# Retention, experts, recurrence, experts on one core: the recurrence's first chunk of returned rows is fetched in the experts' block and taken by halves

## What is computed

```
x = x + attn_a(layernorm(x))          # retention, 16 heads
x = x + ffn(layernorm(x))             # experts, top 2 of 8
x = x + attn_b(layernorm(x))          # recurrence
x = x + ffn(layernorm(x))

# ffn:    acc = sum over the two chosen experts of  weight * (silu(gate) * up) @ w2.T
# attn_b: sx  = shift(x) - x                       # x is the normed input here
#         xxx = x + sx * time_maa_x
#         m   = tanh(xxx @ tm_w1); delta = m @ tm_w2     (five maps)
#         xw, xk, xv, xr, xg = x + sx * (time_maa_wkvrg + delta)
#         r, k, v, g, w from these; scan over tokens; norm by head; * g @ Wo
```

## Time and profile before

| | us |
|---|---|
| median of 3 runs | 1408.81 |
| lowest and highest of them | 1406.04, 1409.01 |
| the profiled execution, its own time | 1404.32 |
| its span in the trace | 1402.5 |
| PE busy | 1148.3 (82%) |
| DVE busy | 907.4 (65%) |
| ACT busy | 617.2 (44%) |
| POOL busy | 547.9 (39%) |

### The profile page before, as it was taken

The page is one execution under the profiler, slowest core; times in us unless marked ns, Lnnn a source line. Parts: engine busy times, 40 slices in busy tenths (PEclk is TensorE's granted clock), DMA queues, the critical chain, the costliest instruction groups (busy, mean ns, idle before and its releaser), DMA issues. The chain is left out here.

```text
span 1402.5 us, 34498 instructions
## 1 busy us (share of the span) xinstructions
PE 1148.3 (82%) x13832; PEld 792.6 (57%) x13832; DVE 907.4 (65%) x1881; ACT 617.2 (44%) x1311; POOL 547.9 (39%) x532
## 2 busy tenths in 40 slices
PE   5999999966399999178989999998987547999960
PEld 3666666644288888124555555555555326888850
DVE  4677776656655665448596886968656276566645
ACT  2333333323255555125556464564735233555547
POOL 1233232312177776232241514325051024777740
PEclk9999999988699999588999999999999777999985
DMA  8032222106923333200101000010000095333338
GB/s 313 2 118 88 69 92 92 61 1 249 328 92 105 101 103 98 75 0 32 32 3 32 4 31 21 15 32 3 2 4 2 2 363 180 103 102 103 104 123 304
DMA packets 62250, 125.65 MB, mean 90 GB/s; under 512 B 7568, under 2 KB 43152, under 8 KB 59152
## 3 DMA queue, kind: packets, MB, share of 16 engines
q1 hardware_dynamic: 48464, 86.20, 17.4%
q0 software_dynamic: 13632, 37.24, 8.5%
HBM read 79.63 MB, written 43.78 MB: 88 GB/s over the span
## 5 line engine op out<-in xcount | busy, mean ns | idle before, releaser
L991 POOL DMA_INDIRECT ffn_xs<-xn_rows,ffn_from_row x142 | 137.7, 970 | 130.2 <-DVE ffn_to_row L1361 78.1
L997 POOL DMA_INDIRECT y_rows<-ffn_ys,ffn_to_row x142 | 140.2, 987 | 53.3 <-issue 33.2
L1146 PE MATMUL ffn_ps_h<-ffn_w_high,ffn_xst 128*128 x568 | 156.7, 397 | 0.2 <-issue 0.2
L1384 DVE TENSOR_TENSOR ffn_act_in<-ffn_silu_g,ffn_ps_h 128x256 f32<-128x256 f32 x142 | 59.9, 422 | 139.5 <-ACT ffn_silu_g L1031 139.5
L1166 PE MATMUL ffn_ps_o<-ffn_w,ffn_act_t 128*128 x284 | 118.3, 440 | 0.5 <-DVE ffn_act_t L1389 0.5
L1031 ACT ACTIVATE ffn_silu_g<-ffn_ps_h 128x256 f32<-128x256 f32 x142 | 54.4, 383 | 145.1 <-PE ffn_ps_h L1146 145.1
L1146 PEld LDWEIGHTS ffn_ps_h<-ffn_w_high,ffn_xst 128*128 128x128 f32 x568 | 98.1, 191 | 19.9 <-issue 0.9
L1723 POOL TENSOR_TENSOR rec_mixed_w<-rec_mixed_w,rec_xnt 128x512 f32<-128x512 f32 x16 | 17.2, 1090 | 218.7 <-DVE rec_mixed_w L2498 218.7
L1146 PE MATMUL ffn_ps_h<-ffn_w_low,ffn_xst 128*128 x284 | 89.3, 396 | 0.0
L548 DVE TENSOR_TENSOR ret_probs<-ret_score,ret_causal 128x2048 f32<-128x2048 f32 x32 | 73.3, 2292 | 21.7 <-PE ret_score L412 21.7
L261 POOL TENSOR_TENSOR ret_roped<-ret_rope_t 128x512 f32<-128x512 f32 x32 | 40.6, 1267 | 105.3 <-DVE ret_rope_t L541 105.3
(11 more groups left out here) (319 smaller groups left out, 2797.5 us busy)
## 6 DMA issues: line engine op xcount, KB each, us to landing
home<-y_rows SPq DMA_DIRECT2D x20, 512.0 KB, 5.2
ffn_w_high<-w_split SPq DMA_DIRECT2D x8, 1024.0 KB, 9.3
ffn_w_low<-w_split SPq DMA_DIRECT2D x8, 1024.0 KB, 10.5
ffn_w<-w_split SPq DMA_DIRECT2D x8, 1024.0 KB, 13.7
ret_w_raw<-in_f_w SPq DMA_DIRECT2D x12, 512.0 KB, 5.6
w_split<-ret_w_high SPq DMA_DIRECT2D x12, 512.0 KB, 2.7
w_split<-ret_w_low SPq DMA_DIRECT2D x12, 512.0 KB, 4.5
xn_rows<-home SPq DMA_DIRECT2D x10, 512.0 KB, 12.3
```

What stands on the lines that cost most here:

```text
L991: pool.indirect_dma_start(xs[:, n % UNROLL, :], None, xn_rows[:], bass.IndirectOffsetOnAxis(ap=from_row[:, n:n + 1], axis=0)) \
L997: pool.indirect_dma_start(y_rows[:], bass.IndirectOffsetOnAxis(ap=to_row[:, m:m + 1], axis=0), ys[:, m % UNROLL, :], None).then_inc(ys_sto ...
L1146: mm = pe.matmul(ps_h[:, u % 2, :], one_pass(xst[:, u % 2, part, k, :]), one_pass(w1[w_part][k][:, bass.ds(e, E_COLUMNS)]), start=(part + ...
L1384: dve.tensor_tensor(act_in[:, u % 2, :], silu_g[:, u % 2, :], ps_h[:, u % 2, FF:2 * FF], ALU.mult) \
```

## The change

1. The fetch of chunk 0 moves from SP's queue in the recurrence to SP's queue at the end of the first experts' block, behind the waits for `ys_stored`, and is cut into four transfers of 256 KB: both choices' rows of tiles 0 and 1, then both of tiles 2 and 3. They count on two new semaphores, `first_rows[0]` and `first_rows[1]`. Nobody waits for them before the barriers.
2. So that the rows have a place that outlives the block, `xn` moves into `home`, which grows by 1024 columns; the experts' normed tiles then lie there in six groups of four rather than five.
3. DVE takes chunk 0 by halves of two tiles (`first_half`): sums, statistics, moments, negated mean, for each half apart. It does this first; clearing `core` and centring the value weights (`centre_values`) now stand behind it.
4. POOL takes the power and the offset for each half (`rstd_of_first`), and its four clearings of tiles stand behind both.
5. ACT norms two tiles when their half is ready. PE transposes each tile when that tile is normed.
6. In the turn n = -1 DVE's `add_ys(1, 0)` stands behind `mix_x(0)` rather than ahead of it.

```diff
@@ experts: SP @@
                 for u in range(UNROLL):
                     sp.wait_ge(ys_stored[u], 16 * len(range(u, NTILES, UNROLL)))
+                if out is None:
+                    for h in range(2):
+                        for s, tile in enumerate(returned_rows(home)):
+                            sp.dma_start(tile[:, 2 * h:2 * h + 2, :],
+                                         y_rows[s * TOKENS:(s + 1) * TOKENS, :].rearrange("(i p) c -> p i c", p=P)[:, 2 * h:2 * h + 2, :]) \
+                                .then_inc(first_rows[h], 16)
...
-HOME = REC_COLUMNS + 4 * C
+HOME = REC_COLUMNS + TOPK * 4 * C
+
+
+def returned_rows(home):
+
+    return [home[:, REC_COLUMNS + s * 4 * C:REC_COLUMNS + (s + 1) * 4 * C].rearrange("p (i c) -> p i c", i=4) for s in range(TOPK)]
...
@@ recurrence: SP @@
-                for c in range(CHUNKS):
-                    if c >= 1:
-
-                        sp.wait_ge(xt_in_psum, c)
-                        sp.wait_ge(ys_added, c * 2 * CT)
+                for c in range(1, CHUNKS):
+
+                    sp.wait_ge(xt_in_psum, c)
+                    sp.wait_ge(ys_added, c * 2 * CT)
...
@@ recurrence: POOL @@
+                def rstd_of_first(h):
+                    own = slice(h * CT // 2, (h + 1) * CT // 2)
+                    pool.wait_ge(first_moments, (h + 1) * (MOMENT_STEPS + 1))
+                    pool.tensor_tensor(rstd[:, own], vare[:, own], expo[:, own], ALU.pow).then_inc(first_rstd, 1)
+                    pool.wait_ge(first_rstd, 2 * h + 1)
+                    pool.tensor_tensor(offset[:, own], mean[:, own], rstd[:, own], ALU.mult).then_inc(first_rstd, 1)
...
@@ recurrence: ACT, norm(c) @@
-                    act.wait_ge(ln_rstd, 2 * (c + 1))
+                    if c >= 1:
+                        act.wait_ge(ln_rstd, 2 * c)
                     for i in range(CT):
+                        if c == 0:
+                            act.wait_ge(first_rstd, 2 * (2 * i // CT + 1))
...
@@ recurrence: PE, transpose_x(c) @@
-                    pe.wait_ge(xn_ready, (c + 1) * CT)
                     if c >= 1:
+                        pe.wait_ge(xn_ready, (c + 1) * CT)
                         pe.wait_ge(r_ready, c)
                     for i in range(CT):
+                        if c == 0:
+                            pe.wait_ge(xn_ready, i + 1)
...
@@ recurrence: DVE @@
+                def first_half(h):
+
+                    half = range(h * CT // 2, (h + 1) * CT // 2)
+                    dve.wait_ge(first_rows[h], 32)
+                    for s, tile in enumerate((xn, second_y)):
+                        for i in half:
+                            if s > 0:
+                                dve.wait_ge(ys_added, h * CT + i - half[0] + 1)
+                            dve.scalar_tensor_tensor(x[:, i, :], tile[:, i, :], weight[:, s, i:i + 1], x[:, i, :],
+                                                     ALU.mult, ALU.add).then_inc(ys_added, 1)
+                    for i in half:
+                        dve.wait_ge(ys_added, h * CT + CT // 2 + i - half[0] + 1)
+                        dve.bn_stats(x_stats[:, i, :], x[:, i, :]).then_inc(first_stats, 1)
...
+                first_half(0)
+                first_half(1)
+                centre_values()
+                for n in range(-1, CHUNKS + 1):
...
-                    if then:
-                        add_ys(n + 2, 0)
-                    if now:
+                        if then:
+                            add_ys(n + 2, 0)
                         k_to_eights(n)
                     if ahead:
                         mix_x(n + 1)
+                    if n == -1:
+                        add_ys(n + 2, 0)
```

73 lines of the change are left out of this document (43 added, 30 removed).

## The result

The changed kernel took 1394.42 us (median of five runs, 1392.49 to 1396.67). The kernel before, timed beside it, took 1406.04 (1404.10 to 1409.01). The ratio, taken from the means of these runs, is 0.9911 with a 95% interval of 0.9897 to 0.9926, a gain of 12.5 us (10.4 to 14.5); the medians themselves lie 11.6 apart.

A forecast was written before the change was run, and what follows sets the result against it. The bound was the serial chain across engines between the first experts and the recurrence. An earlier `sx` (5.6) plus chunk 1's sums (3.75) gave about 9.4 us off the median 1408.81: 1399.4, range 1394.5 to 1405.5.

The forecast's parts named there:

- The fetch: End of the experts' block: SP's four issues take 2.03 us, 1.4 covered, so the barrier opens 0.7 later; bounds 0 and 2.03.
- When DVE can begin: Recurrence start: DVE's first sum at 573.3 us, its own time; the second half's rows land by 575.6 at worst, hidden.
- DVE by halves: DVE on chunk 0: each half takes 3.25 us, both 6.5, ending at 579.8 instead of 582.94.
- POOL, ACT, PE: Chain from DVE's second half to `sx`: 4.3 us remain, so `sx` starts at 584.1, 5.6 earlier.
- Clearing and centring: On DVE behind the halves: 3.0 us, from 579.8 to 582.8, beside POOL, ACT and PE, with 1.3 to spare.
- Chunk 1's sums: DVE, moved behind the first mix: `mix_x` begins 1.25 us behind `sx`'s start instead of 5.00, saving 3.75.
- Who gets in the way: POOL's first power beside DVE's second-half sums: interference taken as 0, bound 1.3 us.
- the power shuts DVE out: Rival: POOL's power and offset delay DVE's second-half sums by 0.75 and 0.2 us; gain 8.4, time 1400.4, chance 0.15.
- SP's transfers hold the barrier until they land: Rival at the barrier: DVE begins at 575.4 to 577.0 us, gain about 6.5, time 1402.3; chance 0.1.
- The sum: 5.6 + 3.75, say 9.4 us gained; PE's first large product at 586.8; profiled execution 1394.9, against the median 1399.4.
- How the numbers follow: Gain of 4.5 to 13 us plus 1.5 at each end for run spread gives 1394.5 to 1405.5; faster 0.92.
- The clock: PE's clock levels: the same work meets level changes elsewhere once the chain moves; taken as 0, 3 us both ways.

The follow-up runs named there:

- e6: The changed kernel with chunk 0 fetched in eight transfers of 128 KB instead of four of 256 KB; ratio to the kernel before 0.996.
- e3: The kernel before with only chunk 0's fetch moved into the experts' block, as two 512 KB transfers, with the larger `home`; ratio to before 0.9982.
- e7: The changed kernel with its four transfers shared between SP's and ACT's queues, two each; ratio to the kernel before 0.9935.
- e8: The changed kernel with its four transfers issued first on SP's queue in the recurrence, not in the experts' block; ratio to the kernel before 0.9957.
- e5: The changed kernel with clearing `core` and centring the value weights ahead of the two halves; ratio to the kernel before 0.9939.
- e4: The changed kernel without halves: DVE, POOL and ACT take chunk 0 whole, the four early transfers stay; ratio to the kernel before 0.9956.
- e1: The kernel before with only chunk 1's first sums moved behind the first mix; 1403.55 us against 1408.49, ratio 0.9979.
- e9: The changed kernel with two fetch queues, `xnt` copy and `sx` by halves, PE starting on half the mix, clearing and centring behind `mix_x`; 1394.57 us, ratio 0.9913.

## Why the prediction was right in its steps and short in its sum

**The fetch.** Four issues took 1.92 (forecast 2.03), and the block starts 6.73 - 5.91 = 0.8 later (forecast 0.7, bounds 0 and 2.03). Right, for the reason given: e6 shows each further issue coming through in full, e3 and e7 show two issues covered. The cover was 1.2 and not 1.4, since SP still waits 0.2 where it is the last; the two semaphores cost 0.07 (e8's block at 5.98 for 5.91).

**When DVE can begin.** The step took DVE's own start of before, 572.59, and added the barrier's 0.7: 573.3, or 7.12 behind the last scatter's issue. It was 6.78. DVE's start of before held 0.5 that belongs to the clearing of `core` in front, as e5 shows by bringing it back. Both halves' rows were in place when DVE wanted them: no wait stands at 572.17 or 575.37. For the second half e4 gives the moment, 8.42 behind the last scatter's issue, which is 573.8 here and within the forecast's 575.6.

**DVE by halves.** 3.20 and 3.28 for the two halves (forecast 3.25 each).

**POOL, ACT, PE.** From the end of DVE's half to `sx` are 582.73 - 578.65 = 4.08; forecast 4.3. The power takes 0.70 and 0.82 for two columns, where I had taken the 1.05 of four. `sx` stands 10.56 behind the first sum; forecast 10.8.

**Clearing and centring.** They end at 582.10, 0.63 ahead of `sx`; forecast 1.3 to spare. Half the cover was eaten by the 0.42 ahead of the clearing and by the chain being shorter. Undone, it costs 3.4 (e5).

**Chunk 1's sums.** 3.75 forecast; from `sx` to the product 3.73 measured, alone in e1 and in the changed kernel (2.73 for 6.46). `mix_x` follows `sx` after 1.26.

**Who gets in the way.** Nobody here: four sums beside the power took 1.67 [575.37 in the timeline after], four without it 1.67 (572.17). The rival that the power shuts DVE out has fallen. The Trainium skill's rule (SBUF — State Buffer, Who interferes with whom) does not hold for the power: it took 0.82 beside the sums for 0.70 alone, and held up none of them. The rule does describe the offset beside `sx` in e9, 0.55 for 0.20 and ending with it.

**SP's transfers hold the barrier until they land.** Fallen: SP's wait at the barrier ended 0.2 behind its last issue, at about 570.1, while none of the four landings took less than 2.7, and in e3 the block began exactly as early as before.

**The sum.** The seam was forecast at 20.6 (586.8 - 566.2) and measured at 20.08, and all four traces of the kernel agree within 0.01. The gain in it is 9.9 for 9.4; the 0.5 is the 0.34 of DVE's start and the 0.2 of the chain.

**The step that failed** is the one from the profiled execution to the time, in "The sum" and "How the numbers follow". I took the median of three runs, 1408.81, as the level of before. Its five runs had 1406.04, the profiled one had 1404.32, and from that one the same sum had given 1394.9, against 1394.42 measured (1392.81 in the changed kernel's profiled execution). Of the miss of 5.0, 1408.81 - 1406.04 = 2.8 is this level; the other 2.2 are a gain of 11.6 between the medians instead of 9.4, of which 0.5 is the seam. The other 1.7 the medians do not place. In the profiled pair, 11.5 apart, 1.7 lies in parts of the program that the change does not touch (0.8 ahead of the seam, 0.9 at the end), and the later sessions put the gain at 9.6 (5.9 to 13.2) and 11.4 (8.6 to 14.2). The range's 1.5 at each end for the spread of three runs was too little: the median of before alone moved from 1406.04 to 1408.49 between sessions, and its single runs lay from 1402.37 to 1416.13.

The range was also added up wrongly. 1408.81 less a gain of 13 and less 1.5 is 1394.3, and 1408.81 less 4.5 and plus 1.5 is 1405.8; the text has 1394.5 and 1405.5. By its own terms the measured 1394.42 lies just inside. That changes nothing in the 2.8 of the level, which is the larger fault.

**The clock** was forecast at 0 with 3 both ways. For this kernel 0 was right, 525.2 behind the seam for 525.1, but not for the reason given. The same work did not meet the changes of level elsewhere: they moved with the chain. The clock rose 5.5 us behind the product's start (5.3 before), fell again at 12.3 (12.2) and stayed down for 6.8 (6.8). That it came out so was luck; for every other arrangement of the seam the stretch was 2 to 12 us longer in the profiled executions, in most of them more than the 3 that I allowed. Why the lower level lasts so differently on the same work stays open.
